# Cross-attention over 98 context tiles: score and weighing matmuls issued tile by tile in turn instead of step by step

## What is computed

```python
def _L0_xattn_ref(enc_outputs, dec_outputs):          # enc: 12544 x 256, dec: 128 x 256
    a_t = jnp.einsum('bed,btd->bet', enc_outputs, dec_outputs)
    a_t = jax.nn.softmax(a_t, axis=-1)                # over the 128 latent rows
    c_t = jnp.einsum('bet,bed->btd', a_t, enc_outputs)
    return c_t

x = x + _L0_xattn_ref(ctx_1024, _layernorm(x, axis=-1))
x = x + _L0_attn_ref(_layernorm(x, axis=-1), L0_attn_w_attn, L0_attn_b_attn, L0_attn_w_proj, L0_attn_b_proj)
x = x + _L0_ffn_ref(_layernorm(x, axis=-1), L0_ffn_W, L0_ffn_b, L0_ffn_V_r, L0_ffn_C)
```

## Time and profile before

| what | value |
|---|---|
| three timed executions | 117.58, 117.73, 119.17 us (median 117.73) |
| profiled execution, its own time | 118.6 us |
| its span, from the first to the last instruction | 116.6 us |
| outside the span | 2.0 us |
| busy in the span: TensorE, VectorE, ScalarE, GpSimd | 91%, 66%, 58%, 55% |
| mean granted TensorE clock | 0.985 |
| share of TensorE in the chain that ended last | 77% |

### The profile page before, as it was taken

One profiled execution on the slowest core, in us unless ns is written; L12 is line 12 of the kernel. 1 busy time (PEld: TensorE's weight loads), 2 busy tenths in 40 slices (PEclk: granted clock), 3 DMA queues, 4 the chain that ended last, 5 costly groups with the idle time before them and its releaser, 6 DMA issues.

```text
span 116.6 us, 2227 instructions
## 1 busy us (share of the span) xinstructions
PE 105.7 (91%) x749; PEld 91.4 (78%) x749; DVE 76.6 (66%) x211; ACT 67.2 (58%) x238; POOL 63.7 (55%) x46
## 2 busy tenths in 40 slices
PE   5788899999999999999999999999979888796980
PEld 1287799999999999999999999999844866694340
DVE  0421999969877788877777777789954347713411
ACT  4037999699878877777777778865200216720000
POOL 7239999879987788877777777783004000000130
PEclk9999999999999999999999999999999999997699
DMA  3999999999999999999999993000000000000001
GB/s 66 351 403 416 413 409 410 401 413 408 409 403 406 413 408 406 412 410 403 408 410 409 398 367 100 3 0 0 0 6 0 0 0 0 0 6 0 0 0 45
DMA packets 8700, 27.73 MB, mean 238 GB/s; under 512 B 1233, under 2 KB 1778, under 8 KB 8690
## 3 DMA queue, kind: packets, MB, share of 16 engines
q1 hardware_dynamic: 8690, 27.60, 60.6%
HBM read 27.46 MB, written 0.13 MB: 237 GB/s over the span
## 4 chain that ended last, share of the span: by engine, by line
PE 77%; DMA 8%; DVE 6%; SPq 3%; ACT 2%; issue 1%; DVEq 0%
PE bank L285 33%; PE bank L296 19%; PE bank L299 10%; DMA cols_ring<-ctx_cols_dram 8%; PE bank L306 2%; PE bank L368 2%; ACT head_exp L456 2%; PE bank L392 2%; PE bank L343 2%; PE bank L376 2%; SPq L210 1%; SPq L205 1%; DVE head_max L571 1%; PE bank L359 1%; PE bank L404 1%
## 5 line engine op out<-in xcount | busy, mean ns | idle before, releaser
L254 POOL TENSOR_TENSOR rows_split<-rows_ring,rows_split 128x1024 fp32r<-128x1024 f32 (+1 forms) x25 | 58.4, 2335 | 16.6 <-ACT rows_split L417 16.6
L285 PE MATMUL bank<-query_t,cols_ring 128*128 128x128 f32 x392 | 48.0, 276 | 1.5 <-DMA cols_ring<-ctx_cols_dram 1.0
L285 PEld LDWEIGHTS bank<-query_t,cols_ring 128*128 128x128 f32 x392 | 45.8, 192 | 3.1 <-DMA cols_ring<-ctx_cols_dram 1.4
L428 ACT ACTIVATE bank<-bank,neg_max 128x128 f32<-128x128 f32 x98 | 33.1, 338 | 12.5 <-DVE neg_max L512 12.5
L296 PE MATMUL bank<-rows_split,probs 128*128 128x512 f32 x98 | 36.9, 412 | 0.0
L417 ACT CAST rows_split<-rows_ring 128x1024 fp32r<-128x1024 f32 (+1 forms) x25 | 25.9, 1034 | 7.9 <-DMA rows_ring<-ctx_rows_dram 7.1
L529 DVE SCALAR_TENSOR_TENSOR probs<-bank,inv_sums,probs 128x128 fp32r<-128x128 f32 x98 | 27.6, 344 | 0.9
L299 PE MATMUL bank<-rows_split,probs 128*128 128x256 f32 x98 | 27.3, 278 | 0.0
L512 DVE TENSOR_REDUCE neg_max<-bank 128x4 f32<-128x512 f32 (+1 forms) x25 | 16.9, 675 | 12.3 <-PE bank L285 12.3
L296 PEld LDWEIGHTS bank<-rows_split,probs 128*128 128x128 f32 x98 | 18.5, 189 | 3.2
L428 ACT ACTIVATION_READ_ACCUMULATOR bank<-bank,neg_max 128x1 f32 x98 | 19.8, 202 | 0.0
(11 more groups left out here) (68 smaller groups left out, 51.9 us busy)
## 6 DMA issues: line engine op xcount, KB each, us to landing
cols_ring<-ctx_cols_dram SPq DMA_DIRECT2D x24, 512.0 KB, 14.9
rows_ring<-ctx_rows_dram SPq DMA_DIRECT2D x24, 512.0 KB, 15.2
wqk_sb<-w_qk_dram SPq DMA_DIRECT2D x1, 512.0 KB
cols_ring<-ctx_cols_dram SPq DMA_DIRECT2D x1, 256.0 KB, 11.1
rows_ring<-ctx_rows_dram SPq DMA_DIRECT2D x1, 256.0 KB, 11.4
wv_sb<-w_v_dram SPq DMA_DIRECT2D x1, 256.0 KB
wproj_sb<-w_proj_dram SPq DMA_DIRECT2D x1, 256.0 KB
wffn_sb<-w_ffn_dram SPq DMA_DIRECT2D x1, 256.0 KB
```

Of the source, the lines that this page charges most:

```text
L254: pool.tensor_tensor(rows_split[:, b, 0:n, 1, :], rows_ring[:, slot * STEP:slot * STEP + n, :], rows_split[:, b, 0:n, 0, :].bitcast(F32), ...
L285: last = pe.matmul(into[:, t * P:(t + 1) * P], cols_ring[:, slot * STEP + t, c, :], query_t[:, c, :], start=(c == 0), stop=(c == DC - 1))
L428: last = act.activation(on[:, t * P:(t + 1) * P], on[:, t * P:(t + 1) * P], ACT.Exp, bias=neg_max[:, b, t:t + 1], accum_out=sums[:, b, t:t ...
```

## The change

On TensorE the waits of a step are taken together at its beginning, first those of the scores of step s, then those of the weighing of step s-3. Then the two kinds of matmuls alternate by tile: four passes of scores of tile 0, the two weighing matmuls of tile 0, and so on. The matmuls themselves, their number, operands and order within a kind stay the same, and so do both semaphores, `scores_ready` behind the last score matmul of the step and `summed` behind its last weighing matmul. No other engine's list is changed.

```diff
-            def score(s):
-                n, slot = tiles_of(s), s % SLOTS
-                into = scores[s % len(scores)]
+            def await_score(s):
+                slot = s % SLOTS
 
                 pe.wait_ge(cols_landed[slot], 16 * (s // SLOTS + 1))
                 if s >= len(scores):
 
                     pe.wait_ge(probs_ready, s - len(scores) + 1)
-                for t in range(n):
-                    for c in range(DC):
-                        last = pe.matmul(into[:, t * P:(t + 1) * P], cols_ring[:, slot * STEP + t, c, :],
-                                         query_t[:, c, :], start=(c == 0), stop=(c == DC - 1))
-                last.then_inc(scores_ready, 1)
-
-            def weigh(s):
-                n, b, pb = tiles_of(s), s % SPLITS, s % PROBS
+
+            def score(s, t):
+                slot, into = s % SLOTS, scores[s % len(scores)]
+                for c in range(DC):
+                    last = pe.matmul(into[:, t * P:(t + 1) * P], cols_ring[:, slot * STEP + t, c, :],
+                                     query_t[:, c, :], start=(c == 0), stop=(c == DC - 1))
+                if t == tiles_of(s) - 1:
+                    last.then_inc(scores_ready, 1)
+
+            def await_weigh(s):
 
                 pe.wait_ge(rows_ready, s + 1)
                 pe.wait_ge(probs_ready, s + 1)
...
+            def weigh(s, t):
+                n, b, pb = tiles_of(s), s % SPLITS, s % PROBS
+                pe.matmul(weighted[:], probs[:, pb, 0, t, :],
+                          rows_split[:, b, t].rearrange("p i d -> p (i d)"),
+                          start=(s == 0 and t == 0), stop=False, skip_group_check=True)
+                last = pe.matmul(weighted[:, 0:D], probs[:, pb, 1, t, :], rows_split[:, b, t, 0, :],
+                                 start=False, stop=(s == STEPS - 1 and t == n - 1), skip_group_check=True)
+                if t == n - 1:
+                    last.then_inc(summed, 1)
...
             for s in range(STEPS + LAG):
                 if s < STEPS:
-                    score(s)
+                    await_score(s)
                 if s >= LAG:
-                    weigh(s - LAG)
+                    await_weigh(s - LAG)
+                for t in range(STEP):
+                    if s < STEPS and t < tiles_of(s):
+                        score(s, t)
+                    if s >= LAG and t < tiles_of(s - LAG):
+                        weigh(s - LAG, t)
```

## The result

The changed kernel takes 1.0186 times as long as the kernel before, with a 95% interval of 1.0123 to 1.0249. The forecast was 120.0 us on 117.73, a ratio of 1.019. The interval lies clear of no change, but on both sides of 2%. In the six executions of each kernel of this comparison the medians are 121.27 us after and 119.06 before; executions of one kernel scatter by up to nine microseconds, and in the profiles of this case the layers behind the loop run at half clock for 0 to 27 us. The experiments are therefore read by what happens in the loop, and a total is given only where it can be compared.

The account below looks back on a forecast made before the run. The prediction took TensorE, never idle in the loop from 13.2 us on, as the bound. Head 1.25, tail 1.03 and alternation 0 gave +2.28 us on 117.73, so 120.0 us, with a range of 118.2 to 121.9.

Parts of the forecast that it names:

- The bound: TensorE in the loop: never idle from 13.2 us on, so a later start of step 3 moves the end equally.
- The alternation at 0: Matmul pace in the loop: alternating by tile neither gains nor loses, a step stays 3.18 us; 0.6 us either way.
- hidden loads: Rival, loop matmuls: a weight load per tile vanishes under the 512 columns, 9.5 us saved, 110.5 us; chance 0.08.
- The head, 1.25: Loop start: step 3's scores wait for step 0's probabilities and start at 14.46 instead of 13.21, 1.25 us late.
- The sum: Whole kernel: head 1.25, tail 1.03 and alternation 0 give +2.28 us, 120.0 us, 1.9% slower.
- The next wait at the head: Step 4: step 1's probabilities come at about 16.9, step 4 is due at 17.6, so no second wait.
- The reserve, 0.76: Mid-loop: probabilities let TensorE go on at 5.60, needed at 6.36; 0.76 us is left, so no wait.
- The tail, 1.03: Loop end: weighing of step 23 waits 1.03 us for its probabilities, some 0.1 of it already ahead of step 22.
- Later loads at 0: Transfers of step s+8: issued at most 2.3 us later, but far ahead of the work, so cost 0.
- Costly changes: Rival, loop: 64 more changes between matmul kinds at 0.075 us each, 124.8 us; chance 0.09, shared with a closed loop.
- A missing wait: Rival, head or tail: one of the two waits is shorter or covered, 118.8 to 119.0 us; chance 0.06.
- The clock at the head: Rival, before step 3: TensorE's 1.8 us rest lowers the clock, 1.7 us more, 121.7 us; chance 0.09.

Follow-up runs that it names:

- e1: Kernel before, its matmul order kept, with both waits moved ahead of the scores; median of four executions 126.74 us, no ratio formed, steps of 3.180 us.
- e10: Kernel before with columns loaded one step ahead of rows and ScalarE's exponents put ahead of the next step's row split; ratio 0.9892 to the kernel before.
- e9: Changed kernel alternating in steps 5 to 21 alone, the other steps in the old order; ratio 0.9955 to the kernel before.
- e5: Kernel before with half of each score matmul's work left out (64 columns a pass instead of 128); steps of 3.180 us.
- e6: Changed kernel with half of each score matmul's work left out (64 columns a pass instead of 128); steps of 3.173 us.
- e2: Changed kernel alternating in steps 4 to 21 alone, steps 3 and 22 to 24 in the old order; median of four executions 124.28 us, no ratio formed.
- e7: Changed kernel alternating more finely within a tile: two score passes, the 512 columns, two score passes, the 256 columns; steps of 3.200 us.
- e3: Changed kernel with the old order up to step 3, alternating from step 4 to the end; ratio 1.0041 to the kernel before.
- e8: Changed kernel with a lag of two steps instead of three between scores and weighing; 206.51 us.
- e11: Kernel before with columns loaded first and ScalarE's two jobs exchanged, plus warming matmuls in TensorE's rests behind the loop; median 116.17 us, ratio 0.9795.

## Why the prediction was right, step by step

- *The bound.* TensorE without a rest from step 3 on, so that a later start moves the end by as much: shown by e1 (step 4 to the add 69.63 with step 4 late by 1.27) and, in the other direction, by e10.
- *The alternation at 0.* Right, and shown by e9; its sign is a small gain, 3.173 instead of 3.180 a step, 0.15 us over the loop. The bound of 0.6 either way held. The argument was that each distance is the longer of a matmul's work and the next one's load. e5 and e6 bear that out, with the load's distance at 0.112. The prediction said against the hidden loads that a pass streams for as long as its load, so that there is nothing to hide. e5 and e6 give a stronger reason: even where the columns are halved and a hidden load would have shown, none was hidden.
- *The head, 1.25.* P0 to step 4 grew by 1.24, and e1 has 1.27 from the place of the wait alone. The sum needed step 3 to be held back by its columns. In the profiles with a slow step 0 it is not: e2, in the old order, starts step 3 at 13.41, and e7, with the waits first, at 14.89, each with P0 near 14.8. There the same wait costs 1.5, so this term differs between executions.
- *The next wait at the head.* The prediction worked out that step 4 would find the probabilities of step 1 in time in the changed kernel, which is so. It did not follow what that means for a repair; e2 and e3 had to show that.
- *The reserve, 0.76.* VectorE ends the probabilities of step 10 at 45.04 + 1.12 = 46.16, and step 13 starts at 47.04: 0.88, less the 0.12 of the release. No wait in mid-loop. With the lag at two, TensorE waits in every step (e8).
- *The tail, 1.03.* The second distance grew by 0.92, and 0.15 of pace was gained in the loop, 0.13 of it behind step 4: the wait itself cost 1.05. The prediction put some 0.1 of it ahead of step 22; it is 0.25 (0.78 ahead of step 23), and the prediction's own rows give that too, 83.64 + 0.12 against 82.26 + 1.25. The sum is untouched by the slip.
- *Later loads at 0.* TensorE waits for columns twice in the changed kernel as before, at the head alone, and never in mid-loop.
- *The sum.* 2.28 was forecast and 2.16 measured in the loop; the difference is the pace.
- *The rivals.* Hidden loads: refuted by e6 and e7. Costly changes: refuted by e9. A missing wait: neither was missing. The clock at the head: not seen in the changed kernel's profile, where it stayed at 1.00 through the rest of 1.78 us, but seen in e6 with half of the score work. The one execution of 128.16 us has no profile, but it does not need a fall in the loop: it lies 8.6 above the kernel's fastest at a mean clock of 0.905, and e3 has executions 8.3 to 8.7 above its fastest, at 0.89 to 0.91, one of them profiled with the loop at 1.00.

## What to carry to other kernels

Where an engine works through its list in order, moving a wait forward is a change of its own: cost it apart from the work that moves with it, at the head and the tail of the loop, where the lag is not yet filled or already runs out. Work that is put in front of a signal delays whoever hangs on that signal, by the length of that work; a reserve hides this in mid-loop and not at the last step, where the chain behind the signal sets the end. Before interleaving two kinds of matmul for their weight loads, look in the trace at how far ahead a load starts. Here no load started before the matmul just ahead of its own, so a long matmul covered one load in either order, and no order gained more than 7 ns a step.

## What was not expected

- Step 0 ran at two paces from execution to execution, its passes 0.112 or 0.213 us apart, behind the same warming matmuls (0.213 in e2 and 0.112 in e3, whose lists are the same up to there).
- An fp32 score pass of 64 columns takes the same 0.112 us as one of 128; a step stays at 3.180 (e5).
- At half of the score work the clock fell in the loop, in e5 during a rest of only 0.56 us before step 3, and stayed low for 6.8 us, although TensorE was busy for 6.14 of 6.50 us. The kernel before has a rest of 0.52 us at the same place and kept 1.00.
- Behind the loop the clock stood at 0.50 for 3 us in the kernel before's profile, and for 27 in those of e1 and e3. The matmuls there are the same, but the fall comes at different places: 10.6 us behind the residual add in e1 and e3, among the head-by-head scores, and 20.5 us behind it in the kernel before, ahead of the projection. What decides between them is open. With 27 us of it these stages take 37.6 us (e3), and 29.6 with none (e7): 8 us, more than three times the effect under study. With fourteen more short warming matmuls in the rests the clock was 0.99 in e11's profile, and at least 0.997 on average in each of its six executions.
